# A chunked gated delta rule beside a Hadamard feed-forward block: two more steps that use all four quadrants of TensorE, and block loads split over two queues

## What is computed

```python
qkvz = (hidden_states @ w_qkvz.T).reshape(Bsz, Sl, NH, 2 * DK + 2 * DV)
...                                          # causal conv of 4 taps over q, k, v; l2 norms; decay g, gate beta
def step(Sstate, xs):
    q_t, k_t, v_t, g_t, b_t = xs
    Sstate = Sstate * jnp.exp(g_t)[..., None, None]
    kv = jnp.einsum('bhk,bhkv->bhv', k_t, Sstate)
    delta = (v_t - kv) * b_t[..., None]
    Sstate = Sstate + k_t[..., :, None] * delta[..., None, :]
    o_t = jnp.einsum('bhk,bhkv->bhv', q_t, Sstate)
    return (Sstate, o_t)
...
o = o * lax.rsqrt(var + EPS) * norm_weight * jax.nn.sigmoid(z)
return o.reshape(Bsz, Sl, VDIM) @ w_out.T
...
x = x + _L0_attn_ref(xn, ...) + _L0_ffn_ref(xn, ...)
```

## Time and profile before

| | us |
|---|---|
| median of 3 runs | 805.7 (802.5, 805.7, 807.76) |
| the profiled execution | 803.39 |
| its span | 801.4 |
| PE busy | 731.8 (91%) |
| PE weight loads | 480.1 (60%) |
| DVE busy | 672.0 (84%) |
| ACT busy | 326.3 (41%) |
| POOL busy | 274.5 (34%) |
| queue of SP's DMAs | 47.93 MB, 27% of the 16 engines' span |

### The profile page before, as it was taken

One profiled execution on the slowest core, in us unless ns is written; L12 is line 12 of the kernel. 1 busy time (PEld: TensorE's weight loads), 2 busy tenths in 40 slices (PEclk: granted clock), 3 DMA queues, 4 the chain that ended last, 5 costly groups with the idle time before them and its releaser, 6 DMA issues.

```text
span 801.4 us, 26961 instructions
## 1 busy us (share of the span) xinstructions
PE 731.8 (91%) x11562; PEld 480.1 (60%) x11562; DVE 672.0 (84%) x1224; ACT 326.3 (41%) x737; POOL 274.5 (34%) x185
## 2 busy tenths in 40 slices
PE   1699899999999999999989999899999999999976
PEld 1445456656666566656666566566566665667564
DVE  4899978889889988897988978798998989896655
ACT  2255234443535344443524335262444435354120
POOL 3034212615251523342160623415072523433411
PEclk9899999999999999999999999899999999999999
DMA  8123230413242231405052141313314140421101
GB/s 231 54 66 99 67 75 2 87 44 78 67 82 49 49 95 25 98 5 102 14 114 49 26 118 20 70 43 64 80 24 106 24 107 18 80 37 16 37 9 54
DMA packets 140407, 49.79 MB, mean 62 GB/s; under 512 B 118145, under 2 KB 131841, under 8 KB 140161
## 3 DMA queue, kind: packets, MB, share of 16 engines
q1 hardware_dynamic: 139664, 47.93, 27.0%
q10 hardware_dynamic: 624, 0.15, 0.2%
HBM read 40.44 MB, written 7.60 MB: 60 GB/s over the span
## 4 chain that ended last, share of the span: by engine, by line
PE 53%; DVE 11%; issue 6%; SPq 4%; DMA 3%; POOL 3%; ACT 2%; DVEq 0%; ACTq 0%; POOLq 0%
PE bank L759 20%; PE bank L850 4%; PE bank L907 4%; DVE kq L260 4%; PE bank L879 3%; PE bank L959 3%; PE bank L848 3%; PE bank L787 3%; PE bank L846 2%; PE bank L823 2%; SPq L711 2%; PE bank L862 2%; PE bank L892 2%; PE bank L780 2%; POOL kqg L1268 2%
## 5 line engine op out<-in xcount | busy, mean ns | idle before, releaser
L759 PE MATMUL bank<-xnT,wq 128*128 128x512 f32 x512 | 254.3, 621 | 4.7 <-DVE kq L260 4.6
L260 DVE SCALAR_TENSOR_TENSOR kq<-bank,cw,kq 128x510 f32<-128x510 f32 (+2 forms) x288 | 212.2, 742 | 15.0 <-ACT kq L1087 12.1
L759 PEld LDWEIGHTS bank<-xnT,wq 128*128 128x128 f32 x512 | 90.1, 192 | 81.5 <-issue 66.1
L1087 ACT ACTIVATE kq<-bank,cw 128x512 f32<-128x512 f32 x96 | 65.9, 687 | 129.0 <-PE bank L759 119.2
L1274 POOL TENSOR_TENSOR Sd<-St,dec 128x256 f32<-128x256 f32 x32 | 20.6, 643 | 262.6 <-DVE St L383 197.8
L1268 POOL TENSOR_TENSOR kqg<-kq,rows 128x1024 f32<-128x1024 f32 x32 | 77.8, 2447 | 57.6 <-DVE kq L260 48.3
L1278 POOL TENSOR_TENSOR ost<-ost,cst 128x8 f32<-128x8 f32 x32 | 54.3, 1696 | 109.6 <-DVE ost L398 109.3
L959 PE MATMUL bank<-wo,oT 128*128 128x256 f32 x256 | 68.2, 383 | 0.2
L371 DVE TENSOR_TENSOR X<-UT,bank 128x256 f32<-128x256 f32 (+1 forms) x96 | 43.4, 461 | 26.9 <-PE bank L850 16.4
L1238 POOL TENSOR_TENSOR stat<-stat,cst 128x16 f32<-128x16 f32 x16 | 46.3, 2894 | 38.6 <-DVE nV L319 38.6
L780 PE MATMUL bank<-xh,wguT 128*128 128x512 f32 x128 | 58.0, 596 | 0.3 <-DVE hf L272 0.3
(11 more groups left out here) (129 smaller groups left out, 1243.4 us busy)
## 6 DMA issues: line engine op xcount, KB each, us to landing
wq<-wqkvz_dram SPq DMA_DIRECT2D x16, 512.0 KB, 3.9
rows<-decay_rows SPq DMA_DIRECT2D x64, 128.0 KB, 3.1
rows<-decay_rows SPq DMA_DIRECT2D x32, 256.0 KB, 4.3
inverse_blocks<-UU SPq DMA_DIRECT2D x32, 128.0 KB
UT<-inverse_blocks SPq DMA_DIRECT2D x128, 32.0 KB, 2.4
wguT<-wgu_dram SPq DMA_DIRECT2D x8, 256.0 KB, 4.2
woraw<-wout_dram SPq DMA_DIRECT2D x16, 128.0 KB, 3.5
base_blocks<-ATP SPq DMA_DIRECT2D x128, 16.0 KB, 1.8
```

The costliest lines, as they stand in the source:

```text
L260: nc.vector.scalar_tensor_tensor(out=y[:, :, t:S], in0=p[:, :, 0:S - t], scalar=cw[:, m, i // 2, 3 - t:4 - t], in1=y[:, :, t:S], op0=ALU.m ...
L759: last = nc.tensor.matmul(ring[i % 2][:], wq[:, q, kc, i // 2, :], xnT[:, kc, (i % 2) * 512:(i % 2) * 512 + 512], start=kc == 0, stop=kc = ...
L1087: nc.scalar.activation(kq[:, i // 2, 2 * (i % 2):2 * (i % 2) + 2, :], split(ring[i % 2][:], 2), ACT.Copy, scale=cw[:, m, i // 2, 3:4]).the ...
```

## The change

Four things:

1. The halves are assigned by the parity of the sequence (`place(h, b)`, b % 2), not by H. A second swap `place2(h, b)` (b % 2 and b // 2 together) is used for the inverse, `nV` and `Y`. `hz.0` reads half h and writes half h ^ H, and its two halves H are one step with their products taken in turn. `delta` reads through `place2` and writes through `place`, into two banks instead of one. `ks` writes through `place2`, and `Y` is now made by two DVE instructions instead of one. `gram.0` works on sequences 0 and 1 and waits for less of the convolution; `turn.0` waits for `d_done`.
2. The factor `root` for H = 1 has to lie in the other halves: a new ACT step `root` copies it with two instructions to `rt`.
3. The tile `UT` has a layout [half H, kind, 8 units, C]. A block row now takes 3 DMAs (2 in the last), and the first block column of X takes 2: 13 DMAs for each half of the partitions. The 13 of h = 0 are issued by SP, the 13 of h = 1 by ACT, each in five steps `uin.0` to `uin.4`, which stand apart in the tables.
4. All order tables are written anew.

```diff
-        UT = tmp("UT", [2, UNITS, C])
-        U16, T16 = UT[:, 0], UT[:, 1]
+        UT = tmp("UT", [2, 2, HALF, C])
+        rt = tmp("rt", [HALF])
...
-        UIN = 16 * 10
+        UIN = 16 * 26
...
-        def place(h, H):
+        def place(h, b):
-            return hs[h ^ H]
+            return hs[h ^ b % 2]
+        def place2(h, b):
+            return hs[h ^ b % 2 ^ b // 2]
...  (DVE)
                 def ks(m, q, c):
                     dve.wait_ge(ks_ready, m * 3 + c)
-                    nc.vector.tensor_tensor(by_half(Y[:]), by_half(nV[:, q, chunk(c)]), sums(), ALU.add).then_inc(y_done, 1)
+                    for j, bs in enumerate((slice(0, 4, 3), slice(1, 3))):
+                        last = nc.vector.tensor_tensor(Y[:, bs], nV[:, q, chunk(c)][:, bs], split(CS[j][:, 0:2 * C], 2), ALU.add)
+                    last.then_inc(y_done, 1)
...  (SP; the same with h = 1 in ACT's program)
+                def uin(m, q, i):
+                    if i == 0:
+                        sp.wait_ge(uu_out, (m + 1) * 32)
+                        wait(sp, hz_done, m * 6)
+                        wait(sp, dl_ready, (m - 1) * 4)
...
+                    h = 0
+                    if i < NB:
+                        at, cols = h * C + i * BASE, slice(i * BASE, i * BASE + BASE)
+                        sp.dma_start(UT[at:at + BASE, 0].rearrange("p k u c -> p (k u) c")[:, :, cols], dub[h, i, 0].rearrange("k u r c -> r (k u) c")).then_inc(ui_in, 16)
+                        sp.dma_start(UT[at:at + BASE, 1, 0, :, cols], dub[1 - h, i, 1, 0].rearrange("u r c -> r u c")).then_inc(ui_in, 16)
+                        if i < NB - 1:
+                            sp.dma_start(UT[at:at + BASE, 1, 1, :, cols], dub[h, i, 1, 1].rearrange("u r c -> r u c")).then_inc(ui_in, 16)
+                    else:
+                        for H in range(2):
+                            sp.dma_start(X[h * C:h * C + BASE, q, half(H), 0:BASE], dub[h ^ H, 0, H, 0].rearrange("u r c -> r u c")).then_inc(ui_in, 16)
...  (PE, hz)
-                        wait(pe, acc_done, m * 4 - 1 + H)
+                        wait(pe, acc_done, m * 4)
...
+                    if j == 0:
+                        for i in range(HALF):
+                            for H in range(2):
+                                for h in range(2):
+                                    last = nc.tensor.matmul(M[H][hs[h ^ H], i * n:i * n + n], ATP[hs[h], q, H * HALF + i, 0, :], UT[hs[h], H, 1, i, 0:n],
+                                                            start=True, stop=True)
+                        last.then_inc(hz_ready, 1)
+                        return
...
-                                last = nc.tensor.matmul(dst, ATP[hs[h], q, u, 0, :], T16[hs[h], u, 0:n], start=True, stop=True)
...  (PE, delta)
-                    for b in range(B):
+                    for b in (0, 2, 1, 3):
                         for h in range(2):
-                            u = b * NCH + c
-                            last = nc.tensor.matmul(CH[hs[h], 256 + b * C:256 + b * C + C], X[hs[h], q, u, :],
-                                                    Y[hs[h], b, :] if c else nV[hs[h], q, u, :], start=True, stop=True)
+                            u, n = b * NCH + c, b % 2
+                            last = nc.tensor.matmul(CS[b // 2][place(h, b), 256 + n * C:256 + n * C + C], X[place2(h, b), q, u, :],
+                                                    Y[place2(h, b), b, :] if c else nV[place2(h, b), q, u, :], start=True, stop=True)
...  (ACT)
+                def root(m, q):
+                    wait(act, nv_done, m * 2)
+                    act.wait_ge(root_done, m + 1)
+                    for h in range(2):
+                        nc.scalar.activation(rt[hs[1 - h], :], stat[hs[h], 2, half(1)], ACT.Copy).then_inc(rt_done, 1)
...  (one row of ACT's new table, around pair 8's loads)
+                     8.vtr.0 9.proj.1 7.delta.0 9.proj.2 8.qsum 8.vtr.1 9.proj.3 7.delta.1 9.ktr.0 7.norm.0 8.root 7.delta.2 9.ktr.1
+                     9.proj.4 7.delta.3 9.proj.5 8.inv.2 9.dec 7.norm.1 8.uin.0 8.uin.1 8.uin.2 9.proj.6 9.proj.7 8.uin.3 8.uin.4 9.ff
```

537 lines of the change are left out of this document (278 added, 259 removed).

## The result

The kernel after takes 797.7 us (median of 20 runs, 790.4 to 806.3), the kernel before 801.8 us in its 20 runs beside it (796.0 to 807.8). The ratio is 0.9935, with a 95% interval of 0.9909 to 0.996: 0.65% or about 5.2 us faster, where 785 us and 2.1 to 2.6% had been forecast. The 5.2 us go by the ratio; the two medians lie 4.1 us apart. So the direction and the range hold, the size does not: of the 18.5 us forecast against the profiled execution (803.4 to 784.9) about a quarter came.

The account below looks back on a forecast made before the run. The prediction took PE's own work as the bound, with DVE close behind at 86%. From the profiled 803.4 us it took 28.5 us of PE work and added 10 us of waits: 784.9, forecast 785 us, range 773 to 802.

Parts of the forecast that it names:

- PE's work, -28.5 us: Four quadrants instead of two save 14.1 us in delta and 14.4 us in hz.0; bounds 15.7 and 30.
- what would show it: Signs for the forecast: PE busy about 703 us, delta rows 0.46 us, hz.0 rows about 1.2 us, ACT near 332.
- The rival of the 48 columns: hz.0's 48-column products gain little in four quadrants: PE loses only 15.7 us, time 793 us; chance 0.10.
- the 25 ns between starts: A least start distance lets delta and hz.0 gain only 8 us, cancelled by added DVE work: 803 us; chance 0.03.
- PE's busy time, about 703 forecast: Sign on the whole kernel: PE's busy time falls from 731.8 to about 703 us; near 716 or more means wrong.
- "What is late next: DVE", +10 us: In the pairs' stages, PE's waits for DVE and ACT, some 20 us, grow by some 10 us; ends 0 and 20.
- The split of Y, +7.5 us "mostly covered": Two DVE instructions for Y between ks and delta add 0.16 us each of 48 times, mostly covered by other PE work.
- The loads, costed at nothing: 26 block loads a pair on SP and ACT land in time for hz.0, costing nothing; late loads (804 to 830) 0.12.
- The slack of 1.4 us: Margin between the block loads' landing (411.0) and the moment hz.0 needs them (412.4).
- the first rival: DVE takes the bound more than allowed: 795 us, or 798 to 803 with only 15.7 us off PE; chance 0.15.

Follow-up runs that it names:

- after_again: The changed kernel run again with no edit: 798.2 us, ratio to the kernel before 0.9947.
- The filled tail: The changed kernel (trace name after_tail_busy) with eight spare 64 x 64 products behind each ks, delta and state of the last pair: 793.9 us, 0.9868 to the kernel before.
- the other fillings: Six spare 128 x 128 products before hz.0's last wait in pairs 4, 8, 13, added to the changed kernel with spare last-pair products: 789.6 us, 0.9828; again 790.4 us, 0.9848.
- the control: The kernel before with the same spare products in its last pair and an added wait for hf_done: 804.2 us, ratio 1.0027 to the kernel before.
- after_two_quadrants: The changed kernel with hz.0 and delta back on two quadrants, all else as changed: 812.1 us, ratio 1.0141 to the kernel before.
- the short taps: Last convolution tap cut to 16 columns in three kernels: before 795.9 us (0.9918), after 790.5 us (0.9863), before with only the quadrants changed 805.0 us (1.0048).
- after_12_loads: The changed kernel with 12 block loads a pair, all on SP and none on ACT: 795.3 us, ratio 0.9906 to the kernel before.
- after_short_tap: The changed kernel with the convolution's last tap on 16 columns: 790.5 us, ratio 0.9863 to the kernel before.
- the two kernels with the quadrants alone: The kernel before with hz.0 and delta on four quadrants, turn.0 moved in 13 pairs: 810.4 us, 1.0085; the same with the last tap on 16 columns: 805.0 us, 1.0048.

## Why the prediction was off

**PE's work, -28.5 us: right.** By the groups `delta` went from 32.3 + 11.0 to 22.8 + 7.4 us, 13.1 less (forecast 14.1), and `hz.0` from 33.5 to 19.1, 14.4 less (forecast 14.4). A `delta` call of 16 records lasts 0.46 us (0.68 before) and an undisturbed `hz.0` 1.15 us (2.08), as the section on what would show it had said:

```profile
370.12 1.15 PE L866 MATMUL bank<-UT,ATP 64*64 64x48 f32 x64
425.61 0.46 PE L904 MATMUL bank<-nV,X 64*64 64x64 f32 x16
```

With a mean of 225 ns for one record, the start distance of `hz.0`'s records is (1.15 - 0.22)/63 = 14.8 ns. The rival of the 48 columns falls, and so does that of the 25 ns between starts, which had reckoned from record to record like the rest of the prediction: the reading of the Trainium skill ("TensorEngine Tiling (Array Packing)", Instruction Overhead) as a least distance between any two starts does not hold for the records of this trace. A product of the program is two records, so that from product to product the distance is 29.6 ns; the trace does not say which of the two the page's overhead would be counted by.

**PE's busy time, about 703 forecast, 709.5 measured.** The groups of `delta` and `hz.0` give 27.5 us, the page only 22.3: other groups became some 3.5 us longer by the sum of their rows. A lower clock on all of PE's other work is a likely part of it, and a term that the sum did not have.

**The granted clock, the missing term.** Its mean is 0.9895 for before (the 79 runs beside the experiments) and 0.978 for after (20 runs, and the same in the 12 of after_again), and within either kernel the time goes up by about 6 us for each 0.01 that the run's mean clock goes down (6.0 in before and 5.5 in after by a straight line through the runs; correlation -0.81 and -0.72). The 0.0115 between the kernels are thus worth, by an estimate from these slopes, some 7 us, about half of the 13 us between forecast (-18.5) and result (-5.2). The filled tail is the test of it: it raised the mean clock to 0.986 and brought 5 to 6 us back (0.9935 and 0.9947 to 0.9868), 7 to 10 us together with the other fillings, while the control brought none. The forecast was made against one execution of before at 0.988 and had no term for after being granted less.

**"What is late next: DVE", +10 us: the size met in one profile by luck, the mechanism wrong.** PE's idle time rose by 10.0 us between the two profiled executions (11.8 between after_two_quadrants and after_again). But it does not come from a fuller DVE, as the short taps show, and it is not the growth by a ratio of idle times that the prediction assumed: the wait for taps fell from 4.6 to 2.1 us, and the growth is in the recurrence, 8.6 to 21.1 us before `delta`, `ks` and `state`. By after_two_quadrants 9.3 of these 12.5 us came with the new order and the split of Y.

The shorter `delta` did not turn into waiting as such. In the last pair, where hardly anything else stands between the steps, `delta` and the `state` behind it, in after_two_quadrants:

```profile
778.23 0.68 PE L904 MATMUL bank<-Y,X 64*64 64x64 f32 x16 [0.61 <-DVE Y L384]
779.45 0.46 PE L915 MATMUL bank<-d,kd 64*64 64x64 f32 x16 [0.54 <-ACT d L1186]
```

and in after_again, in a stretch where its clock is still 1.00:

```profile
769.05 0.46 PE L904 MATMUL bank<-Y,X 64*64 64x64 f32 x16 [0.61 <-DVE Y L384]
770.08 0.46 PE L915 MATMUL bank<-d,kd 64*64 64x64 f32 x16 [0.57 <-ACT d L1186]
```

From start to start it is 1.22 us with two quadrants and 1.03 with four: 0.19 of the 0.22 us come out, and the gap grows by 0.03. What takes them back follows: PE is idle for a larger share of the same chain, and the clock falls there to 0.66 to 0.83 over 20 us, against 0.91 with the long `delta`. From the first `delta` of the last pair to its `ff` it is 14.5 us in after_two_quadrants, 14.6 in after_again, 15.3 in after, and 13.2 in after_tail_busy, where the clock stays at 1.00.

**The split of Y, +7.5 us "mostly covered": not covered.** The instructions take 282 ns each (287 forecast), but one starts before the other's recorded end, so that DVE's busy time for Y rose from 20.0 to 23.1 us and not by 7.5. Even so undoing the split gave about 5 us, with the reserve on four runs and their clock made above. The prediction named the 7.5 us and put nothing into its sum, since PE waited for Y only 2.1 us in the whole run. That small wait did not show that there was room: it is 5.6 us in after, and still 5.0 with Y in one instruction, so most of its rise is the new order's, which was not costed either.

**The wait of `hz.0`, not costed: wrong.** The line `acc_done, m * 4` stood in the diff, and its price in the old order is 7.7 us. How much of it remains in the new order was not measured by itself; the rows show 6.5 us of waiting for yacc in four pairs instead of 4.3 in six, three of the four over 1 us long, and behind such a gap the clock can fall, as it did behind one of the three in after.

**The loads, costed at nothing: right**, with a bound of 2 to 3 us. No wait of PE's products for a load is left, ACT's busy time stayed (325.5 us, 332 forecast), and PE waited for zt once, 1.6 us. The slack of 1.4 us had been reckoned too high: the inverse's last step passes five DVE rows of some 0.68 us (four taps and oT) and two short ones, where the prediction counts six long ones, 4.1 us. By five it is 3.4 us and the slack 0.7. Another slip changes nothing here: 15.7 us off PE with 20 us given back is 803.4 - 15.7 + 20 = 808, not the 803 that the first rival names as its end.

**The whole account**, by ratios: the change without its quadrants costs 11.3 us (of it the split of Y about 5, the loads 0 to 3, and the rest, some 3 to 6 us, the joined wait and the new order, not taken apart), and the quadrants bring 16.5 us instead of 28.5. Of the 12 us lacking there, the mean clock of the two kernels' runs (0.984 and 0.978) explains about 3.5 us by the slope above. The others are not taken apart: 2 to 3 us are added waits in the recurrence, and the interval of each ratio is some 3 to 4 us wide each way.

So these steps of the prediction failed: the sum had no term for a lower clock (about 7 us by the slope), put the split of Y at nothing (about 5 us) and the joined wait and the new order as well (3 to 6 us), and its one term for what comes back, 10 us for DVE as the next bound, stood for a mechanism that the short taps rule out.

**What stays open.** Gaps that the profile puts down to "issue", with nothing waited for, come in some executions and not in others. In after_again, PE in order of time:

```profile
506.07 0.55 PE L875 MATMUL bank<-UT,Q 64*64 64x48 f32 x10
509.44 3.22 PE L875 MATMUL bank<-UT,Q 64*64 64x48 f32 x54 [2.83 <-issue]
```

and the windows over it:

```profile
508.00:512.00 4.00, 2.56 (x48) 2.56 (x50) 0.55 (x1) 0.00 (x0) 0.00 (x0) 0.61 0.31 35
512.00:516.00 4.00, 4.00 (x16) 1.67 (x12) 2.75 (x2) 0.00 (x0) 0.00 (x0) 0.53 0.35 73
```

The clock is at 0.61 and 0.53 behind it. Such a gap inside `hz.1` of pair 9, of 1.0 to 2.8 us, stands in seven of the sixteen traces (before, after_again, after_12_loads, after_short_tap, after_tail_busy and the two kernels with the quadrants alone) and is not there in the others, after among them. Why PE stood there is not known. It is likely one reason for the spread of 2% between runs, and why a difference of the size of this change's effect must be read from medians.

## What to carry to other kernels

When work is taken off an engine, look at the stretch where it is already waiting between short steps. There the shorter step did shorten the chain (0.19 of 0.22 us), but it left PE idle for a larger share of the time, and the clock that it was granted fell. When two steps are joined into one, every wait of both moves to the joint start: price that line of the diff as its own term. When all order tables are written anew, run the new order without the gain that it is for: here that one experiment showed where most of the new waits came from. Read the granted clock stretch by stretch together with the busy time, over several executions; where it is low at the same place in all of them, as in the last recurrence here, a few spare products can be worth more than they cost, and where it is low in some of them only, a single pair of traces proves nothing. And look at what else a control's edit does: the spare products in before came with a wait of 1.9 us.
